# Silu of the gate rewritten with tanh, at steps of its own, in an attention and feed-forward kernel

## Chip, cores and metric
One core of a Trainium2 chip runs the whole program. The metric is the device time of one execution in microseconds (us); lower is better.

## What is computed
Inputs are x (4 batches of 1024 tokens, width 256), the attention weights Wq, Wk, Wv, Wo and the feed-forward weights w1, w2 with biases. Cut to what matters:

```python
xn = _layernorm(x, axis=-1)
s = _L0_attn_ref(xn, Wq, Wk, Wv, Wo)      # 16 heads of 16, 8 key heads, causal,
                                          # last 128 tokens or a landmark token
g = _silu(_L0_ffn_ref(xn, w1, b1, w2, b2))
# _L0_ffn_ref: h = gelu(xn @ w1_q.T + b1); h @ w2_q.T + b2, with w1_q, w2_q in {-1, 0, 1}
x = x + s * g
```

With z the output of the feed-forward part, the gate is silu(z) = z / (1 + exp(-z)) = z/2 (1 + tanh(z/2)).

## The kernel before
The program is written engine by engine, with semaphores set by hand. After a setup come five turns: one that only prepares batch 0, then one for each batch ("turn 0" to "turn 3"; `turn` in the code). Turns 0 to 2 do the attention of their batch and also prepare the next batch (`prep`); turns 1 to 3 first finish the second half of the batch before (`prev`).

A turn walks through 48 steps (`STEPS`). A step is one block of 128 keys (`kb`) for one group of 4 heads (`g`) and one chunk of 512 queries (`c`): 4 groups of 4 steps for chunk 0 (steps 0 to 15), 4 groups of 8 for chunk 1 (steps 16 to 47; `C1` is 16). In step i:
- PE does `scores(i, 0)`, `values(i - 2)`, `scores(i, 1)` (lines 735 and 742 for the scores and their mask, 755 for the values). `scores(i, u)` waits until the exponentials of step i - 1, half u, are done.
- ACT does `exps(i)`: for each half one or two exponentials from PSUM to the tile probs (lines 829 and 832), 128x1024 when the block lies before the diagonal.
- DVE copies out a finished group (`group_out`), and does the small work.

Between the steps stand jobs, in an order that the list `jobs_of` fixes by step numbers; each engine walks the same list and does its part. `ffn_up` is 8 blocks of the first feed-forward product (PE, line 672), each followed by a gelu on ACT into the tile `hid` (line 790) and by a split into h_hi and h_lo on DVE and POOL (lines 899, 904, 867). Those of chunk 1 stand just before step 16, those of the next batch's chunk 0 at the turn's end. `ffn_down` (PE, line 682) is spread over steps 6 to 13 and 34 to 41; its output plus bias is written by DVE to the tile `gate` (line 911, the "z add"; semaphore z_done). `out_proj` (PE, line 690) at steps 27 to 32, and at steps 4 and 5 of the next turn, is multiplied with the gate by DVE (line 919), and POOL adds x (line 863). `mean_row` (line 714) and `transpose` (line 696) prepare the next batch at steps 16 to 18; `v_proj` (line 709) stands at the turn's end, and ACT copies it out (line 806).

`gates(c)` on ACT (line 818) turns z into the gate in place: one Silu over 128x1024 for a chunk. It stands ahead of `exps(16)` for chunk 0, and behind the gelus at the turn's end for chunk 1:

```python
act.wait_ge(z_done, TC * (c + 1))
act.activation(gate[:, :, :], gate[:, :, :], ACT.Silu).then_inc(gate_done, 1)
```

Exp, Gelu and Silu each make the compiler place an ACT_TABLE_LOAD when the one before was of another kind. The first 1024 columns of `hid` also serve as `x_prev`, in which the second half of the batch before gets its residual at steps 4 and 5 and from which it is sent out.

Of the kernel before, what the change touches and what calls it, by code (L numbers as in the profile page):

```python
# [9 lines left out]
ALU = mybir.AluOpType  # L30
ACT = mybir.ActivationFunctionType
# [11 lines left out]
TC = CH // P  # L43


def kernel_program(nc, x, Wq, Wk, Wv, Wo, w1, b1, w2, b2, out):
# [5 lines left out]
    FT = F // P  # L52
# [36 lines left out]
    with ExitStack() as ctx:  # L89
# [3 lines left out]
        def sem(name):  # L93
# [67 lines left out]

        x_prev = hid[:, :, :].rearrange("p a n -> p (a n)")[:, 0:TC * D].rearrange("p (t d) -> p t d", d=D)
        head_block = x_prev[:, 0, 0:P]
        w_tmp = probs[:, 2].rearrange("p a n -> p (a n)")
# [27 lines left out]
            sem(n) for n in ("att_out", "att_in", "rden_done", "rden_in", "attT_done"))  # L192
        hid_split, hi_done, hid_split_pool, z_done, gate_done, prod_done, y_done, xres_in, y_out = (
            sem(n) for n in ("hid_split", "hi_done", "hid_split_pool", "z_done", "gate_done", "prod_done", "y_done", "xres_in", "y_out"))
        xprev_in, w_first = sem("xprev_in"), sem("w_first")
# [306 lines left out]
        DOTS_AT, RANK_AT = 6, 19  # L502
        LN_AT = 5

        def jobs_of(main, prep, prev):
# [33 lines left out]
        def turn(b, main, prep, prev, x_next):  # L539
# [30 lines left out]
            with nc.Block(no_gpsimd_drain=True) as block:  # L570
# [207 lines left out]
                def _(act):  # L778
                    def job(n, kind, *a):
                        bank, before_it = bank_of[n]  # L780
                        ps = aux_ps[:, bank, :]
                        if kind == "ffn_up":
                            c, f, u = a
                            act.wait_ge(aux_done, n + 1)
                            if u >= NHID:

                                act.wait_ge([hid_split, hid_split_pool][(u - NHID) % 2], (u - NHID) // 2 + 1)
                            if u == 0 and prev:
                                act.wait_ge(y_out, 16)
                            act.activation(hid[:, u % NHID, :], ps, ACT.Gelu, bias=b1_sb[:, f:f + 1]).then_inc(aux_free[bank], 1)  # L790
# [24 lines left out]
                    def gates(c):  # L815

                        act.wait_ge(z_done, TC * (c + 1))
                        act.activation(gate[:, :, :], gate[:, :, :], ACT.Silu).then_inc(gate_done, 1)

# [16 lines left out]
                    for i in range(NSTEP if main else last_step + 1):  # L836
                        for j in jobs_at(i - 0.5, i):
                            job(*j)
                        if main and i == C1:
                            gates(0)  # L840
                        if main:
                            exps(i)
                        for j in jobs_at(i, i + 0.5):
                            job(*j)
                    if main:
                        tail = jobs_at(NSTEP - 0.5, 999)
                        first = [j for j in tail if j[1] == "ffn_up"]
                        for j in first:
                            job(*j)
                        gates(1)  # L850
                        for j in tail[len(first):]:
                            job(*j)
# [24 lines left out]
                def _(dve):  # L877
# [14 lines left out]
                    def job(n, kind, *a):  # L892
# [21 lines left out]
                        elif kind == "out_proj":  # L914
                            t, u = a
                            dve.wait_ge(aux_done, n + 1)
                            if u >= n_prev and t % TC == 0:
                                dve.wait_ge(gate_done, t // TC + 1)
                            dve.tensor_tensor(gate[:, t % TC, :], ps[:, 0:D], gate[:, t % TC, :], ALU.mult).then_inc(prod_done, 1)  # L919
                            dve.wait_ge(prod_done, u + 1)  # L920
# [33 lines left out]
                        elif kind == "dilate":  # L954
                            dve.wait_ge(aux_done, n + 1)
                            dve.tensor_scalar(landmark[:, :], ps[:, 0:T], 1.0, None, ALU.min).then_inc(aux_free[bank], 1)
                            dve.wait_ge(aux_free[bank], before_it + 1)

                    def normalise_x(t):
# [72 lines left out]
                    for i in range(last_step + 1 if not main else NSTEP + LAG):  # L1032
# [4 lines left out]
                        if main:  # L1037
# [7 lines left out]
                            if i == C1 + 8:  # L1045
                                normalise_heads(own)
                            if not prep and i == GROUP_END[5] + LAG + 4:
                                reciprocals(own + 1)
# [56 lines left out]
```

## Time and profile before
| what | value |
|---|---|
| median of 3 runs (lowest, highest) | 742.63 us (741.88, 743.72) |
| span of the profiled execution | 740.2 us |
| PE busy | 632.2 us (85%) |
| PE weight loads busy | 357.2 us (48%) |
| DVE busy | 374.9 us (51%) |
| ACT busy | 475.4 us (64%) |
| POOL busy | 88.3 us (12%) |
| mean granted clock of PE | 0.922 |

The span is from the first to the last instruction of one profiled execution; the page gives no other time for it. The median of the runs is 2.4 us above that span. Busy shares are over the whole span; the granted clock is a share of full speed (1.00 is 2.4 GHz, 0.50 is 1.2 GHz).

### The profile page before, as it was taken

The page shows a single profiled execution, that of the slowest core. Times are in us where ns is not written, and L with a number is a line of the kernel's source. Part 1 is how long each engine was busy: PE and PEld are TensorE (multiplying, and loading weights), DVE is VectorE, ACT ScalarE, POOL GpSimd, SP SyncE. Part 2 cuts the span into 40 slices and gives each one's busy share as a digit, 9 for nine tenths or more (in the row PEclk, how much of TensorE's full clock was granted, in tenths as well). Part 3 has the DMA queues.
Part 4 walks back from the last instruction along what each step waited for, and adds up shares of the span by engine and source line. Part 5 has one row for each costly group of instructions (what it writes and reads, how often), then busy time and mean ns, then how long its engine had stood idle before and what let it go on. Part 6 is the DMA issues. An engine that isn't in the chain of part 4 may idle for free. (4 is left out here: it accounts for less than half of the span.)

```text
span 740.2 us, 11752 instructions
## 1 busy us (share of the span) xinstructions
PE 632.2 (85%) x4336; PEld 357.2 (48%) x4336; DVE 374.9 (51%) x1000; ACT 475.4 (64%) x723; POOL 88.3 (12%) x94
## 2 busy tenths in 40 slices
PE   1226866999999979999999769999999899799982
PEld 1215752664455456554454636654554556334532
DVE  4976972574827444676545615748364521410101
ACT  1021245678776866687778655697768656888680
POOL 5600020020010021020100201110100210201001
PEclk9656776999999999999999969999999799899996
DMA  7000298200127359001091748001082690020101
GB/s 213 0 0 1 40 115 135 43 8 9 58 36 94 53 79 203 20 7 31 30 107 31 95 130 113 12 8 57 23 108 40 83 157 15 8 89 8 51 10 49
DMA packets 46833, 43.84 MB, mean 59 GB/s; under 512 B 6065, under 2 KB 41394, under 8 KB 46770
## 3 DMA queue, kind: packets, MB, share of 16 engines
q1 hardware_dynamic: 44642, 41.18, 33.4%
q10 hardware_dynamic: 2128, 1.84, 0.8%
q8 instruction: 38, 0.62, 0.4%
q14 instruction: 25, 0.20, 0.1%
HBM read 11.28 MB, written 4.19 MB: 21 GB/s over the span
## 5 line engine op out<-in xcount | busy, mean ns | idle before, releaser
L829 ACT ACTIVATE probs<-sc_ps,shift 128x512 f32<-128x512 f32 (+1 forms) x288 | 175.6, 616 | 98.7 <-PE sc_ps L742 98.0
L735 PE MATMUL sc_ps<-q_stack,k_stack 99*128 99x512 bf16 (+3 forms) x768 | 197.3, 342 | 29.3 <-PEq L209 10.2
L832 ACT ACTIVATE probs<-sc_ps,key_bias 128x1024 f32<-128x1024 f32 (+3 forms) x256 | 204.6, 817 | 16.9 <-PE sc_ps L735 16.3
L755 PE MATMUL att_ps<-probs,v_sb 128*32 128x512 f32 (+3 forms) x1536 | 165.6, 503 | 0.0
L735 PEld LDWEIGHTS sc_ps<-q_stack,k_stack 99*128 99x128 bf16 x768 | 49.9, 99 | 177.2 <-ACT probs L832 65.0
L742 PE MATMUL sc_ps<-near_mask,mask_ident 128*128 128x256 bf16 (+1 forms) x576 | 103.8, 264 | 0.0
L867 POOL TENSOR_TENSOR h_lo<-hid,h_hi 128x512 fp32r<-128x512 f32 x32 | 43.1, 1347 | 338.4 <-DVE h_hi L899 338.4
L742 PEld LDWEIGHTS sc_ps<-near_mask,mask_ident 128*128 128x128 bf16 x576 | 55.7, 101 | 36.8 <-issue 6.7
L682 PE MATMUL aux_ps<-w2T,h_hi 128*128 128x256 f32 x256 | 70.1, 307 | 0.0
L682 PE MATMUL aux_ps<-w2T,h_lo 128*128 128x256 f32 x256 | 63.2, 279 | 0.0
L790 ACT ACTIVATE hid<-aux_ps,b_sb 128x512 f32<-128x512 f32 x64 | 43.0, 687 | 22.5 <-PE aux_ps L672 14.7
L672 PE MATMUL aux_ps<-xT_hi,w1T 128*128 128x512 f32 x128 | 54.8, 428 | 2.7 <-ACT hid L790 2.7
L899 DVE CAST h_hi<-hid 128x512 fp32r<-128x512 f32 x64 | 30.7, 492 | 45.0 <-ACT hid L790 44.8
L755 PEld LDWEIGHTS att_ps<-probs,v_sb 128*32 128x32 f32 x1536 | 30.4, 108 | 47.3 <-issue 31.3
L672 PE MATMUL aux_ps<-xT_lo,w1T 128*128 128x512 f32 x128 | 51.3, 401 | 0.0
L911 DVE TENSOR_TENSOR gate<-aux_ps,b_bc 128x256 f32<-128x256 f32 x32 | 13.6, 424 | 73.7 <-PE aux_ps L682 53.0
L1013 DVE COPY att_raw<-att_ps 128x512 f32<-128x512 f32 x32 | 22.1, 691 | 56.4 <-PE att_ps L755 34.8
L682 PEld LDWEIGHTS aux_ps<-w2T,h_hi 128*128 128x128 f32 x256 | 48.1, 188 | 1.9
L682 PEld LDWEIGHTS aux_ps<-w2T,h_lo 128*128 128x128 f32 x256 | 48.4, 189 | 0.3
L919 DVE TENSOR_TENSOR gate<-aux_ps,gate 128x256 f32<-128x256 f32 x32 | 13.6, 424 | 59.6 <-PE aux_ps L690 59.6
L690 PE MATMUL aux_ps<-wo_sb,attT 128*128 128x256 f32 x128 | 34.3, 403 | 10.3 <-DVE attT L1025 10.3
L863 POOL TENSOR_TENSOR xn<-xn,gate 128x256 f32<-128x256 f32 x20 | 14.6, 729 | 221.7 <-DVE gate L919 221.5
(152 smaller groups left out, 776.8 us busy)
## 6 DMA issues: line engine op xcount, KB each, us to landing
q_stack<-q_parts SPq DMA_DIRECT2D x96, 128.0 KB, 8.2
k_stack<-k_parts SPq DMA_DIRECT2D x24, 256.0 KB, 8.8
xn<-in_L_attn_hidden_states SPq DMA_DIRECT2D x4, 1024.0 KB, 9.2
attT<-att_raw SPq DMA_DIRECT2D x128, 32.0 KB
rden_bc<-den SPq DMA_DIRECT2D x64, 64.0 KB
probs<-in_L_ffn_w SPq DMA_DIRECT2D x2, 1024.0 KB, 7.7
out_y<-xn SPq DMA_DIRECT2D x4, 512.0 KB, 6.5
xn<-in_L_attn_hidden_states SPq DMA_DIRECT2D x3, 512.0 KB, 4.0
```

Of the source, the lines that this page charges most:

```text
L672: last = pe.matmul(ps, w1T[:, k, f * P:(f + 1) * P], part[:, k, c * CH:(c + 1) * CH], start=(k == 0 and part is xT_hi), stop=(k == KD - 1 ...
L682: last = pe.matmul(ps[:, 0:D], part[:, f, q * P:(q + 1) * P], w2T[:, f, :], start=(f == 0 and part is h_hi), stop=(f == FT - 1 and part is ...
L690: last = pe.matmul(ps[:, 0:D], attT[:, k, q * P:(q + 1) * P], wo_sb[:, k, :], start=(k == 0), stop=(k == KD - 1))
L735: last = pe.matmul(sc_ps[:, 2 * u + hh, lo:CH], k_stack[0:KROWS + SHIFT_ROWS, h // REP, kb * P:(kb + 1) * P], q_stack[0:KROWS + SHIFT_ROWS ...
L742: last = pe.matmul(sc_ps[:, 2 * u + hh, lo:near], mask_ident[:, :], near_mask[:, first:end:kb + 1, :], start=False, stop=True)
L755: last = pe.matmul(att_ps[32 * q:32 * q + 32, n % 2, lo:CH], v_sb[:, kb, j * VW:j * VW + 32], probs[:, i % 3, q, lo:CH], start=(kb == 0), ...
L790: act.activation(hid[:, u % NHID, :], ps, ACT.Gelu, bias=b1_sb[:, f:f + 1]).then_inc(aux_free[bank], 1)
L829: last = act.activation(probs[:, i % 3, us, lo:near], sc_ps[:, us, lo:near], ACT.Exp, bias=shift[:, 0:1], scale=HD ** -0.5)
L832: last = act.activation(probs[:, i % 3, us, near:CH], sc_ps[:, us, near:CH], ACT.Exp, bias=key_bias[:, kb:kb + 1], scale=HD ** -0.5)
L867: pool.tensor_tensor(h_lo[:, f, :], hid[:, u % NHID, :], h_hi[:, f, :].bitcast(F32), ALU.subtract).then_inc(hid_split_pool, 1)
L899: ins = dve.tensor_copy(h_hi[:, f, :], whole)
L1013: dve.tensor_copy(att_raw[:, :], att_ps[:, n % 2, :]).then_inc(att_out, 1)
```

## The change
The Silu becomes a tanh of z/2 on ACT into the first 1024 columns of hid (`half_tanh`), and a product (1 + tanh) * z on DVE; the factor 1/2 is applied where the out-projection is multiplied with the gate. Both stand at steps of their own: the tanh of chunk 0 before `exps(14)`, that of chunk 1 before `exps(44)`, and the products one step later on DVE. The first gelu of each block waits for the product, since it overwrites hid. The wait for the output DMA of x_prev moves from the first gelu to the first tanh.

```diff
+        half_tanh = hid[:, :, :].rearrange("p a n -> p (a n)")[:, 0:TC * D].rearrange("p (t d) -> p t d", d=D)
...
+        GATES_AT = (14, C1 + 28)
...
-                            if u == 0 and prev:
-                                act.wait_ge(y_out, 16)
+                            if main and u % FT == 0:
+
+                                act.wait_ge(gate_done, u // FT + 1)
...
                     def gates(c):
 
                         act.wait_ge(z_done, TC * (c + 1))
-                        act.activation(gate[:, :, :], gate[:, :, :], ACT.Silu).then_inc(gate_done, 1)
+                        if c == 0 and prev:
+                            act.wait_ge(y_out, 16)
+                        act.activation(half_tanh[:, :, :], gate[:, :, :], ACT.Tanh, scale=0.5).then_inc(tanh_done, 1)
...
-                        if main and i == C1:
+                        if main and i == GATES_AT[0]:
                             gates(0)
+                        if main and i == GATES_AT[1]:
+                            gates(1)
...
-                        for j in first:
-                            job(*j)
-                        gates(1)
-                        for j in tail[len(first):]:
+                        for j in first + tail[len(first):]:
                             job(*j)
...
-                            dve.tensor_tensor(gate[:, t % TC, :], ps[:, 0:D], gate[:, t % TC, :], ALU.mult).then_inc(prod_done, 1)
+                            dve.scalar_tensor_tensor(gate[:, t % TC, :], ps[:, 0:D], 0.5, gate[:, t % TC, :],
+                                                     ALU.mult, ALU.mult).then_inc(prod_done, 1)
...
+                    def gates(c):
+
+
+                        dve.wait_ge(tanh_done, c + 1)
+                        dve.scalar_tensor_tensor(gate[:, :, :], half_tanh[:, :, :], 1.0, gate[:, :, :],
+                                                 ALU.add, ALU.mult).then_inc(gate_done, 1)
...
+                            if i == GATES_AT[0] + 1:
+                                gates(0)
+                            if i == GATES_AT[1] + 1:
+                                gates(1)
```

ACT around the chunk boundary of turn 3, before (`probs` is written by an exponential, `hid` by a gelu, `gate` by the Silu):

```order
L829 ACTIVATE probs<-sc_ps,shift 128x2x256
L832 ACTIVATE probs<-sc_ps,key_bias 128x2x128
L829 ACTIVATE probs<-sc_ps,shift 128x2x256 x2
L829 ACTIVATE probs<-sc_ps,shift 128x2x128 x2
L790 ACT_TABLE_LOAD
L790 ACTIVATE hid<-aux_ps,b_sb 128x512 x8
L818 ACT_TABLE_LOAD
L818 ACTIVATE gate<-gate 128x1024
L832 ACT_TABLE_LOAD
L832 ACTIVATE probs<-sc_ps,key_bias 128x1024 x6
```

And with the change, at the same place (line 803 is the tanh, 773 the gelu, 814 and 817 the exponentials):

```order
L814 ACTIVATE probs<-sc_ps,shift 128x2x256
L817 ACTIVATE probs<-sc_ps,key_bias 128x2x128
L803 ACTIVATE hid<-gate 128x1024
L814 ACTIVATE probs<-sc_ps,shift 128x2x256 x2
L814 ACTIVATE probs<-sc_ps,shift 128x2x128 x2
L773 ACT_TABLE_LOAD
L773 ACTIVATE hid<-aux_ps,b_sb 128x512 x8
L817 ACT_TABLE_LOAD
L817 ACTIVATE probs<-sc_ps,key_bias 128x1024 x6
```

The tanh stands between the exponentials of steps 13 and 14 with no table load, and between gelus and exponentials one load is left of two. ACT at step 44 of turn 3 with the change:

```order
L817 ACTIVATE probs<-sc_ps,key_bias 128x2x384
L803 ACTIVATE hid<-gate 128x1024
L814 ACTIVATE probs<-sc_ps,shift 128x2x256
L817 ACTIVATE probs<-sc_ps,key_bias 128x2x256
L814 ACTIVATE probs<-sc_ps,shift 128x2x256
```

Before, the two exponentials of 128x2x384 and 128x2x256 (steps 43 and 44) followed each other. DVE at step 15 of a turn that prepares a batch, with the change (line 948 is the product, 883 the cast of the first gelu's output):

```order
L895 TENSOR_TENSOR gate<-aux_ps,b_bc 128x256
L1005 COPY att_raw<-att_ps 128x512
L953 TENSOR_SCALAR xn<-xn,mv,rstd 128x256 x2
L956 SCALAR_TENSOR_TENSOR resid,ssq<-xn 128x256 x2
L948 SCALAR_TENSOR_TENSOR gate<-hid,gate 128x1024
L883 CAST h_hi<-hid 128x512
L888 TENSOR_TENSOR h_lo<-hid,h_hi 128x512
L883 CAST h_hi<-hid 128x512 x2
```

The product stands alone between the normalisation of x and the first cast of the gelu block, where nothing stood before.

## Rows read from the trace of the kernel before
**Rows 1.** Groups of ACT: line, operation, count | busy us, mean ns | idle before
```profile
L818 ACT ACT_TABLE_LOAD x8 | 10.3, 1283 | 0.1
L818 ACT ACTIVATE gate<-gate 128x1024 f32<-128x1024 f32 x8 | 8.5, 1059 | 0.1
```
**Rows 2.** Timeline of ACT, boundary of turn 3: start us, us, instruction, count [idle before]
```profile
636.64 1.27 ACT L790 ACTIVATE hid<-aux_ps,b_sb 128x512 f32<-128x512 f32 x2 [0.94 <-POOL h_lo L867]
637.92 1.28 ACT L818 ACT_TABLE_LOAD   x1
639.22 1.06 ACT L818 ACTIVATE gate<-gate 128x1024 f32<-128x1024 f32 x1
...
641.59 2.12 ACT L832 ACTIVATE probs<-sc_ps,key_bias 128x1024 f32<-128x1024 f32 x2
```
**Rows 3.** Timeline of PE at the same place
```profile
642.75 1.03 PE L735 MATMUL sc_ps<-q_stack,k_stack 99*128 99x512 bf16 x2 [4.25 <-ACT probs L832]
```
**Rows 4.** Windows: busy us (count) by engine, granted clock of PE, DMA share, GB/s
```profile
642.00:643.00 1.00, 0.25 (x1) 0.13 (x2) 0.00 (x0) 1.00 (x2) 0.00 (x0) 0.60 0.00 0
...
649.00:650.00 1.00, 1.00 (x9) 0.35 (x10) 0.59 (x1) 0.93 (x1) 0.00 (x0) 0.98 0.01 2
...
723.00:724.00 1.00, 0.00 (x0) 0.00 (x0) 0.00 (x0) 0.00 (x0) 0.00 (x0) 1.00 0.18 41
```
**Rows 5.** Timeline of ACT in turn 3: step 19, then steps 24 to 27
```profile
650.08 0.47 ACT L829 ACTIVATE probs<-sc_ps,shift 128x256 f32<-128x256 f32 x1
...
660.30 5.17 ACT L832 ACTIVATE probs<-sc_ps,key_bias 128x1024 f32<-128x1024 f32 x5
...
666.71 0.47 ACT L829 ACTIVATE probs<-sc_ps,shift 128x256 f32<-128x256 f32 x1
```
**Rows 6.** Boundary of turn 0: timeline of PE and ACT, and one window
```profile
165.56 3.62 PE L714 MATMUL aux_ps<-xn,ones 128*128 128x256 f32 x16
...
168.88 5.13 ACT L832 ACTIVATE probs<-sc_ps,key_bias 128x1024 f32<-128x1024 f32 x5
174.24 1.11 ACT L832 ACTIVATE probs<-sc_ps,key_bias 128x1024 f32<-128x1024 f32 x1 [0.22 <-PE sc_ps L735]
...
168.00:172.00 4.00, 3.92 (x30) 2.56 (x28) 2.50 (x4) 3.99 (x5) 0.44 (x1) 1.00 0.00 0
```
**Rows 7.** Timeline: ACT at the end of turn 0, PE at the program's end
```profile
266.82 0.78 ACT L806 ACTIVATE v_sb<-aux_ps 128x128 f32<-128x128 f32 x4 [1.78 <-PE aux_ps L709]
...
730.17 5.34 PE L690 MATMUL aux_ps<-wo_sb,attT 128*128 128x256 f32 x14 [10.28 <-DVE attT L1025]
```
**Rows 8.** Timeline of ACT and PE, steps 44 and 45 of turn 0
```profile
244.59 0.69 ACT L829 ACTIVATE probs<-sc_ps,shift 128x512 f32<-128x512 f32 x1
245.16 0.70 ACT L832 ACTIVATE probs<-sc_ps,key_bias 128x512 f32<-128x512 f32 x1
...
246.06 0.48 PE L735 MATMUL sc_ps<-q_stack,k_stack 99*128 99x384 bf16 x2
```
**Rows 9.** Timeline of DVE, ACT and PE, steps 13 to 16 of turn 0
```profile
152.31 0.43 DVE L911 TENSOR_TENSOR gate<-aux_ps,b_bc 128x256 f32<-128x256 f32 x1 [1.58 <-PE aux_ps L682]
152.75 0.69 ACT L829 ACTIVATE probs<-sc_ps,shift 128x512 f32<-128x512 f32 x1 [0.41 <-PE sc_ps L742]
154.03 0.28 PE L735 MATMUL sc_ps<-q_stack,k_stack 99*128 99x128 bf16 x2
155.58 0.47 ACT L829 ACTIVATE probs<-sc_ps,shift 128x256 f32<-128x256 f32 x1 [0.29 <-PE sc_ps L742]
158.15 0.43 DVE L899 CAST h_hi<-hid 128x512 fp32r<-128x512 f32 x1 [3.06 <-ACT hid L790]
```
**Rows 10.** Groups of DVE, columns as in rows 1
```profile
L1025 DVE TENSOR_TENSOR attT<-attT,rden_bc 128x1024 f32<-128x1024 f32 (+1 forms) x9 | 10.0, 1107 | 31.8 <-DMA rden_bc<-den 31.5
L919 DVE TENSOR_TENSOR gate<-aux_ps,gate 128x256 f32<-128x256 f32 x32 | 13.6, 424 | 59.6 <-PE aux_ps L690 59.6
L964 DVE SCALAR_TENSOR_TENSOR resid<-xn 128x256 f32<-128x256 f32 x32 | 12.3, 423 | 0.6
```

More of the change, by code:

```diff
@@ L192, in kernel_program @@
             sem(n) for n in ("att_out", "att_in", "rden_done", "rden_in", "attT_done"))
-        hid_split, hi_done, hid_split_pool, z_done, gate_done, prod_done, y_done, xres_in, y_out = (
-            sem(n) for n in ("hid_split", "hi_done", "hid_split_pool", "z_done", "gate_done", "prod_done", "y_done", "xres_in", "y_out"))
+        hid_split, hi_done, hid_split_pool, z_done, gate_done, tanh_done, prod_done, y_done, xres_in, y_out = (
+            sem(n) for n in ("hid_split", "hi_done", "hid_split_pool", "z_done", "gate_done", "tanh_done", "prod_done", "y_done", "xres_in", "y_out"))
         xprev_in, w_first = sem("xprev_in"), sem("w_first")
```

## The prediction, made before the changed kernel had been run
> **What bounds the kernel now.** I read the page first: PE is busy for 85% of the span and ACT for 64%, so ACT as a whole is not the bound, and only places where the two engines hand work to each other can matter. The second view is the grouped instructions of ACT: 8 Silu instructions of 1.06 us, each with a table load of 1.28 us of its own [rows 1]. Together with what they force (the load that brings the exponential back) this is what the change touches. The third view is the timeline, read at the four kinds of place where a Silu stands now or a tanh will stand: the chunk boundary (step 16) in the turns that prepare the next batch, the same in the last turn, the end of a turn, and the new steps 14 and 44. In what follows "turn 0" to "turn 3" are the four turns with attention.
>
> **The boundary in turn 3** is the one place where the Silu is exposed. The last two gelus end at 637.91, then come load, Silu, load, and the first exponential starts at 641.59, 3.67 us after the first load began [rows 2]. PE stands still for 4.25 us on that exponential [rows 3]. It costs twice: the granted clock is 0.60 in the mean of the microsecond from 642, then half, and is back only in the one from 649 (0.98) [rows 4]. At 1.2 GHz PE can't keep up with ACT: from the first exponential of step 16 to the first of step 19, six of the 1024-wide kind, it takes 650.08 - 641.59 = 8.49 us. The same six at 2.4 GHz, one head group later and again with no other work between, take 666.71 - 660.30 = 6.41 us [rows 5].
>
> **The boundary in turns 0 to 2** looks the same on ACT, but PE has other work there: the mean row (16 matmuls, 3.62 us from 165.56) and the transposes for the next batch. PE is busy for 3.92 of the 4 us from 168 to 172. ACT, released by its last load, starts at 168.88, does five exponentials without a gap, and at 174.24 is again waiting for PE (0.22) [rows 6]. So the Silu is hidden under PE's own queue.
>
> **The end of a turn**: the Silu of the second chunk stands between the gelus and the copies of v. The second group of v copies waited 1.78 us for PE [rows 7], so that Silu is hidden too. In turn 3 it runs while PE sits out 10.28 us for the last attention group's DMA round trips [rows 7].
>
> **What is removed.** Eight loads and eight Silus. The listing of ACT shows no load ahead of a tanh, so 8 x 1.28 = 10.3 us of loads go [rows 1]. Only those of the turn 3 boundary are on the path: 3.67 us there becomes one load with its 1.30 us to the next start (637.92 to 639.22) [rows 2], so **-2.37 us**. The other seven Silus and loads were hidden and give 0; the cover is PE's 3.62 us of mean row plus transposes in three of them, and PE's v projection or the DMA chain in four. With the exponential 2.37 us earlier PE idles 4.25 - 2.37 = 1.9 us. Does the clock fall then? In the trace it stays at 1.00 until 724 at the program's end although PE stopped shortly before 720 [rows 4, 7], so it outlived some 4 us of idleness there, and it fell at the boundary only near the end of a stop of 4.25 us. I take it as kept: 8.49 - 6.41 = **-2.08 us**. Bounds: 0 (it falls all the same) and -2.1 (it stays).
>
> The Trainium skill, ScalarE: Activation LUTs, section What ACT_TABLE_LOAD costs, puts a switch of table sets at about 1283 ns of load and about 1380 ns of drain. The trace doesn't agree with the second part: the load starts 0.01 us after the last gelu's end and the Silu 1.30 us after the load's start [rows 2]. By the page the turn 3 boundary would win 1.36 us more; by the row it wins nothing more.
>
> **What is added on ACT.** A tanh of 128x1024 has no row. The nearest is the Silu of the same tile, 1.06 us; back-to-back instructions overlap by 0.12 us (0.69 us from 244.59, next start 245.16) [rows 1, 8], so it holds the exponentials up by 0.95 us. Ends: 0.69 us (the 512-wide exponential) and 1.06.
>
> Step 44: ACT has no gap there. The first pair of step 44 starts at 244.59, at once behind step 43, and ends at 245.86; PE's first scores of step 45, which wait for that, start at 246.06 [rows 8]. The slack is 0.20 us. PE then goes from scores to values to scores without a wait that could absorb it, and the gelus at the turn's end start from ACT's last exponential. So 0.95 - 0.20 = 0.75 us in each of 4 turns: **+3.0 us**. Ends 0 and 0.95 each.
>
> Step 14: the tanh needs the last z add, which ends at 152.74 on DVE; until then ACT was free. With the tanh first, the exponential of step 14 starts about 153.75 instead of 152.75, 1.0 us later. PE's scores of step 15 wait for its end, 153.44 before, 154.44 after, and stood at 154.03 [rows 9]. That is 0.41 us, and all behind it (values, scores, the gelus' table load, the gelu block) is back to back. 4 turns: **+1.6 us**. Ends 0 and 1.0 each.
>
> **What is added on DVE.** Eight products of 128x1024. No row shows this one; the 128x1024 product of attT takes 1.1 us in the mean [rows 10], so some 9 us of busy time. At step 15 DVE is idle for 3.06 us before the first gelu's cast at 158.15 [rows 9]; queued behind the product is just that cast, and the gelu itself, which now waits for the product (since the tanh uses the tile hid). The product can end near 156.3; ACT's last exponential ends at 156.05, the table load takes it to 157.3, and both come 0.4 later now [rows 1, 9]. At step 45 DVE has nothing but the cast behind the product either, and that waits for the gelus of the turn's end. Cost 0 at both, up to 1.1 us a turn if that cover were gone. The out-projection's product becomes scalar_tensor_tensor: 0.424 us now, against 0.423 for that operation on the same shape [rows 10]: 0. The wait for the output DMA moves from the gelu (step 16) to the tanh (step 14); that DMA is issued once the residuals of steps 4 and 5 are done, nine steps earlier, so 0. POOL and SP keep their order.
>
> **Sum** against the profiled execution (740.2): 3.0 + 1.6 - 2.37 - 2.08 = +0.15, so a span of about 740.4. The three runs have a median of 742.63, 2.4 us above that span; with the same distance **742.8 us**. What a measurement of this kernel can tell from no change is about 0.3%, 2.2 us: from 740.4 to 744.9 is "the same". The three runs alone lie 1.8 us apart, which is of the size of the clock's cold stretches at the start of a turn.
>
> **The rivals.**
> - *The clock falls all the same* (slower). PE's stop at the turn 3 boundary is cut from 4.25 to 1.9 us, not removed, and nothing in the trace has a stop of that length at full clock to compare. From the point at which 1.9 us is enough to lose it, the 2.08 us stay lost: 744.9. For it: the granted clock did fall before the 4.25 us were over. Against: the program's end. 0.14.
> - *The product holds the gelus.* If DVE's product ends after ACT's last exponential of step 15 (156.05) by more than the delay, load and gelus start later, and the whole gelu block with them: up to 1.1 us in each of 4 turns, 747.2. It needs the normalisation of x ahead of it on DVE to run later than it did. 0.05.
> - *The tanhs are absorbed* (faster). If gaps of ACT like the 0.41 and 0.29 us of steps 14 and 15 [rows 9] took them up at both places, +4.6 becomes some +1.6 and the time 739.8. Against: PE waits for ACT there, the gaps are PE's lateness handed on. 0.10.
> - *The Silu was exposed at every boundary.* Then 3 x 2.37 more: 735.7. For it: the three loads and Silus in a row on ACT. Against: PE's full windows [rows 6]. 0.06.
> - *A switch costs a drain as well.* As a mechanism of this kernel: were the activation ahead of a load to give its result up only after a drain that the rows don't show, the boundary of turn 3 would win about as much again as one load, 1.3 us: 741.5. 0.05. This is the page's rule above.
> - That the change doesn't do what it says (a load still stands before the tanh) is excluded by the listing.
>
> **How the numbers follow.** The forecast has 0.60, its own range is 741.3 to 744.4 (the ends of one term moved at a time, and the spread of runs). The time is its value, 742.8. The range reaches to the absorbed tanhs below and the lost clock above: 739.6 to 745.2; outside are the exposed Silus and the held gelus. Faster: 0.10 + 0.06 + 0.02 of the forecast = 0.18. Slower: 0.14 + 0.05 + 0.02 = 0.21, where the lost clock lies on the bound. Same: 0.61.
>
> **What would show it.** In the changed profile: 18 table loads instead of 26. At turn 3's boundary one load and then an exponential, PE idle about 1.9 us there, and the granted clock at 1.00 through the next 8 us. From the gelus' table load at the boundary to that at the turn's end turns 0 to 2 take 0.75 us more than before; from the last z add ahead of step 14 to the boundary's load 0.4 more. The copies of v still wait for PE, and longer. I am wrong if the stretch from step 16 to step 43 in turns 0 to 2 gets shorter by more than 0.3 us, if PE's scores of step 45 don't move against step 43, or if the clock in turn 3 falls.

## The result and the profile after

| | before | after |
|---|---|---|
| median of the runs (lowest, highest) | 742.25 us (741.25, 743.72), 4 runs | 748.77 us (746.29, 750.03), 4 runs |
| span of the profiled execution | 740.2 us | 746.7 us |
| ACT busy | 475.4 us | 464.9 us (62%) |
| DVE busy | 374.9 us | 384.5 us (51%) |
| PE busy | 632.2 us | 629.4 us (84%) |
| mean granted clock of PE | 0.922 | 0.936 |

The ratio is 1.008, 95% interval 1.0059 to 1.0102: 6.5 us slower, where 742.8 was forecast and 745.2 was the upper end. The engine that was relieved did get 10.5 us of its work off (475.4 to 464.9), TensorE ran at a slightly higher clock, and the program is longer. A second and larger comparison (e6 below, 12 runs against 23) put the ratio at 1.0045 (1.0024 to 1.0065). Both intervals lie above 1; the first four runs and the profiled execution lie at the dear end of what the changed kernel does. One execution in the comparisons below, e3's fifth, took 3265 us and is in no ratio.

The groups of the new instructions, columns as in [rows 1] (of ACT, then of DVE):

```profile
L773 ACT ACT_TABLE_LOAD x8 | 10.3, 1283 | 0.1
L803 ACT ACTIVATE hid<-gate 128x1024 f32<-128x1024 f32 x8 | 8.4, 1055 | 3.7 <-DVE gate L895 3.7
...
L903 DVE SCALAR_TENSOR_TENSOR gate<-aux_ps,gate 128x256 f32<-128x256 f32 x32 | 13.6, 424 | 60.3 <-PE aux_ps L672 60.3
L948 DVE SCALAR_TENSOR_TENSOR gate<-hid,gate 128x1024 f32<-128x1024 f32 x8 | 9.8, 1226 | 5.5 <-ACT hid L803 5.3
```

The tanh costs what the Silu cost (1055 against 1059 ns), the out-projection's product is unchanged (424 ns, [rows 10]). The product (1 + tanh) z takes 1226 ns, a little over the 1.1 us that was taken. New is the last column of the tanh: ScalarE stood idle for 3.7 us ahead of it, waiting for VectorE's z add.

**Cutting the time at marks.** To see where 6.5 us come from I cut both traces at the same instructions: the first exponential's table load of a turn ("start"), the turn's first z add, at step 7 ("z1"; the expectations below call it the z add of tile 1), the gelus' table load at the boundary, the gelus' table load at the turn's end, and in turn 3 the exponential's load at the boundary and the end. Each entry is the difference of two start times. The last two columns are second profiles of the same two kernels (e5, e6).

| stretch, us | before | after | before again | after again |
|---|---|---|---|---|
| start to z1, turns 0 / 1 / 2 / 3 | 19.29 / 21.18 / 28.15 / 22.68 | 20.51 / 21.06 / 29.37 / 22.91 | 19.34 / 21.16 / 29.87 / 23.35 | 20.54 / 20.97 / 29.07 / 22.71 |
| z1 to the boundary's load, turns 0 / 1 / 2 / 3 | 19.97 / 19.98 / 19.98 / 20.04 | 20.40 / **23.49** / 20.40 / 20.41 | 19.98 / 19.99 / 19.99 / 20.05 | 20.40 / **21.26** / 20.40 / 20.40 |
| boundary's load to that of the turn's end, turns 0 / 1 / 2 | 96.40 / 96.41 / 96.41 | 97.01 / 97.03 / 97.03 | 96.42 / 96.41 / 96.42 | 96.99 / 97.02 / 96.99 |
| turn 3: boundary's load to the exponential's | 11.45 | 9.10 | 11.45 | 9.08 |
| turn 3: from there to the end | 99.91 | 99.42 | 98.06 | 101.52 |

Of the 6.5 us, the boundary of turn 3 gives back 2.35. Step 14 takes 0.43 + 0.42 + 0.37 in turns 0, 2 and 3 and **3.51 in turn 1**. Step 44 takes 0.61 + 0.62 + 0.62 in turns 0 to 2, and in turn 3 it lies within the last line, whose sum is -0.49. From a turn's end load to the next start it is +0.25 in sum. The rest, +2.55 us, lies in the first line, ahead of any tanh. Of that last item turn 2's 1.2 us are not the change's: the kernel before, profiled again, shows 29.87 us there instead of 28.15, and 93.72 in sum instead of 91.30. The profile on which the prediction was built was a lucky one there. Turn 0's 1.2 us are another matter: the second profiles repeat them (19.34 against 20.54), although they lie ahead of the turn's first tanh. What sets them is open; it is not the work nearby, since e8 and e10 (below), which differ only by matmuls in turn 3, have 19.38 and 20.77 (e12, the same kernel as e10, 20.59).

The windows of that stretch show how it moves. Of turn 2, before and then before again (columns: busy us of PE, its weight loads, DVE, ACT, POOL, then PE's granted clock, DMA share, GB/s):

```profile
424.52:452.67 28.15, 21.38 (x146) 11.58 (x147) 6.46 (x15) 14.86 (x25) 2.91 (x4) 0.77 0.67 124
```

```profile
424.81:454.68 29.87, 22.85 (x146) 11.96 (x147) 6.47 (x15) 14.88 (x25) 2.91 (x4) 0.73 0.70 134
```

It is the same 146 matmul rows in 21.4 us or in 22.9 us of PE, with a mean granted clock of 0.77 or 0.73.

**Turn 1** is the finding of this trace. DVE first, at step 9 and at the last z add:

```profile
302.74 0.69 DVE L1005 COPY att_raw<-att_ps 128x512 f32<-128x512 f32 x1 [3.90 <-DMA den<-att_raw]
...
311.30 0.42 DVE L895 TENSOR_TENSOR gate<-aux_ps,b_bc 128x256 f32<-128x256 f32 x1
```

Then ACT at step 14, PE at step 15, and two windows behind it, all of the same execution:

```profile
311.76 1.06 ACT L803 ACTIVATE hid<-gate 128x1024 f32<-128x1024 f32 x1 [2.54 <-DVE gate L895]
...
313.45 0.28 PE L717 MATMUL sc_ps<-q_stack,k_stack 99*128 99x128 bf16 x2 [2.37 <-ACT probs L814]
...
313.00:314.00 1.00, 0.55 (x8) 0.36 (x12) 0.96 (x4) 0.97 (x2) 0.00 (x0) 0.80 0.11 23
314.00:315.00 1.00, 1.00 (x8) 0.08 (x8) 0.96 (x3) 0.47 (x1) 0.00 (x0) 0.50 0.19 43
```

DVE's copy of the second attention group has to wait until the DMAs of the first group have read the one tile att_raw. It waits 3.90 us. Behind it on DVE stand the layer norm's root, the normalisation of x and two z adds; DVE hardly pauses from there on, and the last z add starts 18.33 us behind z1 (311.30 - 292.97) where the trace of before has 16.20 (306.93 - 290.73). The tanh waits for it, all exponentials of step 14 wait behind the tanh, PE stands for 2.37 us, and on top the granted clock falls at 313.6, 2.5 us after PE had stopped. The kernel before had the same wait (1.37 us in this turn, 2.38 in its second profile), and nobody on ACT needed z before step 16.

Step 44 in turn 0, timeline of ACT:

```profile
246.21 1.05 ACT L803 ACTIVATE hid<-gate 128x1024 f32<-128x1024 f32 x1
247.15 0.69 ACT L814 ACTIVATE probs<-sc_ps,shift 128x512 f32<-128x512 f32 x1
```

The exponential comes 0.94 us behind the tanh's start (0.95 was taken), and 0.61 to 0.62 us of it reach the turn's end.

**Turn 3's boundary**, as [rows 2 to 4]: timeline of ACT, of PE, and windows.

```profile
646.00 1.27 ACT L773 ACTIVATE hid<-aux_ps,b_sb 128x512 f32<-128x512 f32 x2 [0.96 <-POOL h_lo L851]
647.28 1.28 ACT L817 ACT_TABLE_LOAD   x1
648.58 4.13 ACT L817 ACTIVATE probs<-sc_ps,key_bias 128x1024 f32<-128x1024 f32 x4
...
656.40 0.47 ACT L814 ACTIVATE probs<-sc_ps,shift 128x256 f32<-128x256 f32 x1
...
649.74 0.61 PE L717 MATMUL sc_ps<-q_stack,k_stack 99*128 99x512 bf16 x2 [1.90 <-ACT probs L817]
...
651.00:652.00 1.00, 0.60 (x3) 0.13 (x2) 0.46 (x1) 1.00 (x2) 0.00 (x0) 0.76 0.00 0
652.00:653.00 1.00, 1.00 (x6) 0.20 (x8) 0.00 (x0) 0.82 (x2) 0.00 (x0) 0.50 0.15 33
...
655.00:656.00 1.00, 1.00 (x10) 0.52 (x12) 0.27 (x1) 0.61 (x1) 0.00 (x0) 1.00 0.03 8
```

One load instead of two and the Silu; PE idle for 1.90 us, as forecast. But the granted clock falls to half all the same, at 651.5, 3.7 us after PE had stopped (it was busy again by then), and is back at 654.9. The six wide exponentials take 656.40 - 648.58 = 7.82 us, not 6.41.

### The profile page after: what moved, and what is told of

It is laid out like the page before. It is cut to its first block and busy times, and to the rows that moved or that the text cites. A ratio compares the mean times of both kernels' runs of the same rounds, so it can differ in the third digit from the quotient of the medians.

```text
span 746.7 us, 11756 instructions
## 1 busy us (share of the span) xinstructions
PE 629.4 (84%) x4336; PEld 351.8 (47%) x4336; DVE 384.5 (51%) x1008; ACT 464.9 (62%) x715; POOL 87.7 (12%) x94
## 5 line engine op out<-in xcount | busy, mean ns | idle before, releaser
L737 PE MATMUL att_ps<-probs,v_sb 128*32 128x512 f32 (+3 forms) x1536 | 167.8, 509 | 0.0
L883 DVE CAST h_hi<-hid 128x512 fp32r<-128x512 f32 x64 | 33.5, 538 | 36.3 <-ACT hid L773 35.8
L903 DVE SCALAR_TENSOR_TENSOR gate<-aux_ps,gate 128x256 f32<-128x256 f32 x32 | 13.6, 424 | 60.3 <-PE aux_ps L672 60.3
```

The source lines that it names most:

```text
L737: last = pe.matmul(att_ps[32 * q:32 * q + 32, n % 2, lo:CH], v_sb[:, kb, j * VW:j * VW + 32], probs[:, i % 3, q, lo:CH], start=(kb == 0), ...
L883: ins = dve.tensor_copy(h_hi[:, f, :], whole)
```

## The experiments

Theory A: the added time sits at the two tanhs (0.4 us at step 14, 0.6 at step 44, each four times), plus VectorE's lateness, which step 14 puts on the path in turn 1. The rivals: B, it is only how the cold clock falls at the turns' starts; C, step 14 or 44 costs more than its row says. All ratios are against runs of the kernel before on the same chip; a difference in us is the ratio's times the median of before there (743.1 to 743.7).

### e1 and e2: each half of the change alone

```diff
 e1: chunk 0 as before the change, chunk 1 with tanh
-                        if main and i == GATES_AT[0]:
-                            gates(0)
+                        if main and i == C1:
+                            silu(0)
 e2: chunk 1 as before the change, chunk 0 with tanh
-                        if main and i == GATES_AT[1]:
-                            gates(1)
...
                        for j in first:
                            job(*j)
+                        silu(1)
```

> Chunk 0 has its Silu back at the boundary, only the tanh at step 44 and its product stay. Theory A (the added time comes from the two places where a tanh stands ahead of an exponential, and of these mostly from step 14): step 44 costs 0.62 us in each of 4 turns as in the trace of the changed kernel, so +2.5 us against before, about 744.8, and the way from a turn's start to the boundary's gelu load is as before. Rival B (the added time is the clock's cold stretches at the starts of turns, which any change of phase moves): a time anywhere from 741 to 749, with differences sitting ahead of step 9 and not at the tanh. Rival C (step 44 is the costly place by something the trace does not show): over +4 us.

> Only the tanh at step 14 and its product stay, chunk 1 has its Silu back at the turn's end. Theory A: what is left of the changed kernel's +6.5 us without 4 x 0.62, so +4.0 us against before, about 746.3, with the last z add and the tanh in turn 1 late by some 2.5 us. Rival C: under +2.5 us. Theory A also asks that this one and e1 add up to the whole change within 1 us; rival B gives no such sum.

Measured: **e1 746.32 us, ratio 1.0035 (1.0017 to 1.0054)**, +2.6 us as expected; **e2 743.87, ratio 1.0007 (0.9997 to 1.0017)**, +0.5 us where +4.0 was expected. Boundary to turn's end is 97.02, 97.04 and 97.03 us in e1 and 96.40, 96.40 and 96.39 in e2; z1 to the boundary's load is 19.98 three times and 20.05 in e1, and 20.39 to 20.40 in all four turns of e2. So both prices stand exactly where theory A has them, and e2 misses its number mainly because its profile lacks the 3 us of turn 1: its DVE waited 0.22 us there for something else and not for the DMA. The two add to +3.1 us, less than the +6.5 of the first comparison. Rival B is half right: e1 has 94.6 us in its four starts and e2 95.4, with no tanh near them.

### e3: VectorE's wait taken away

```diff
+        def raw_of(n):
+            return hid[:, 2, :] if n == 1 else att_raw[:, :]
...
-                        if n >= 1:
+                        if n >= 2:
                             dve.wait_ge(att_in, 16 * (NQ + 1) * n)
-                        dve.tensor_copy(att_raw[:, :], att_ps[:, n % 2, :]).then_inc(att_out, 1)
+                        dve.tensor_copy(raw_of(n), att_ps[:, n % 2, :]).then_inc(att_out, 1)
```

> The changed kernel, but the second attention group's copy out of PSUM goes to a free third of hid instead of att_raw, so that VectorE doesn't wait there for the DMA that reads the first group's copy. Theory A (the tanh of turn 1 is late because VectorE, in order, stands behind that DMA): VectorE's wait of 3.9 us at step 9 of turn 1 goes, the z adds come in time, and the stretch to the boundary's load falls by some 2.5 to 3 us in turn 1 and by little elsewhere: about 746 us. Rival D (the z adds wait for TensorE's ffn_down sums, not for this DMA): no change, 748.8. Rival B: turn 1 keeps its extra 3 us ahead of step 9.

Measured: 747.91 us, ratio 1.0062 (1.0033 to 1.009). In its trace z1 to the boundary's load is 20.40, 20.41, 20.40 and 20.40 us: turn 1 is like the others, and no wait for the DMA is left at step 9. The missing wait is the edit's doing and not luck, as the table below lets one see: the transfers ahead of the first group's landed later than in e6 (6.70 us behind z1 against 6.35), where DVE waited 2.63 us. The total doesn't show a gain over the changed kernel (e6, 1.0045); the intervals overlap, and in this profile the stretch from turn 3's exponential load to the end took 101.65 us (99.42 in after). By total time e3 is inconclusive, and its number, 746, was missed.

The traces of the other kernels settle the mechanism, since each is one more sample of that wait in turn 1. The second column tells where the wait comes from: it is when the last of the 12 transfers into q_stack, which the turn's start issues, has landed, in us behind z1. The transfers that read att_raw stand behind them and the output's transfer in the same queue.

| kernel | last q_stack transfer landed | DVE's wait for the DMA | last z add behind z1 | tanh at step 14? | z1 to the boundary's load |
|---|---|---|---|---|---|
| e12 | 3.57 | none | 16.20 | no | 19.98 |
| before | 5.24 | 1.37 | 16.20 | no | 19.98 |
| e1 | 5.98 | 2.05 | 16.49 | no | 19.98 |
| before again (e5) | 6.39 | 2.38 | 16.83 | no | 19.99 |
| e8 | 7.18 | 3.54 | 17.98 | no | 19.99 |
| e2 | 3.36 | none | 16.20 | yes | 20.39 |
| e3 (copy to another tile) | 6.70 | none | 16.20 | yes | 20.40 |
| after again (e6) | 6.35 | 2.63 | 17.07 | yes | 21.26 |
| after | 7.85 | 3.90 | 18.33 | yes | 23.49 |

VectorE has some 1.76 us to spare: the last z add is late by the wait less that (2.38 - 1.76 = 0.62, and 16.83 - 16.20 = 0.63; 3.90 - 1.76 = 2.14, and 2.13). Without a tanh at step 14 a late z costs nothing (e8, late by 1.77 us), with it it costs all of it, and in the worst case the clock as well. The late z is probably in part the other side of a gain: where turn 1's start was short (21.0 to 21.4 us) and the copy was not moved, DVE waited 1.4 to 3.9 us, and where it was long (21.8 to 23.1 us), 0 to 1.6 us, in all thirteen such profiles.

### e4 and e9: the tanh ahead of the gelus

```diff
 e4
-                        if main and i == GATES_AT[0]:
-                            gates(0)
...
                         if main:
                             exps(i)
+                        if main and i == C1 - 1:
+                            gates(0)
 e9: the same, and the tanh of chunk 0 written to rden_bc, which is idle then
-                            if main and u % FT == 0:
-                                act.wait_ge(gate_done, u // FT + 1)
+                            if main and u == FT:
+                                act.wait_ge(gate_done, 2)
```

> The changed kernel, but the chunk 0 tanh stands behind the exponentials of step 15, just ahead of the gelus' table load, and the product follows it. Theory A: the z adds are done by then in every turn, so the wait for them goes and the tanh costs its bare 0.95 us four times: turn 1 falls by 2.5 us, turn 3 rises by 0.4, and the sum is 4 x 0.95 + 4 x 0.62 - 3.0 (turn 3's boundary) = +3.3 us against before, about 745.6. The product (1.23 us) is covered by the table load (1.28 us). Rival E (the product holds the gelus): one further us in each turn, 749.6. Rival B: no relation to where the tanh stands.

> e4 with the chunk 0 tanh written to rden_bc instead of hid, so that no gelu waits for the product (the tanh still stands behind the exponentials of step 15). In e4 the gelus' table load, which carries the gelu's wait, stood 1.41 us for the product in each turn, and the gelu block then took 10.28 us to the exponential's load instead of 9.09. Rival E of e4 (the product holds the gelus): both go, 4 x (1.41 + 1.2) = -10.4 us against e4's +14.8, so about +4 us against before; from the z add of tile 1 to the boundary's load 20.9 us in every turn, turn 1 too, however late VectorE is. The other reading (a tanh just ahead of the gelus starves TensorE by itself): over +8 us.

Measured: **e4 758.54 us, ratio 1.0203 (1.0179 to 1.0226)**, +15 us where I had written +3.3; **e9 747.23, ratio 1.0047 (1.0033 to 1.0062)**, +3.5. The two timelines of ACT, e4 and then e9:

```profile
157.13 1.05 ACT L803 ACTIVATE hid<-gate 128x1024 f32<-128x1024 f32 x1
159.58 1.28 ACT L773 ACT_TABLE_LOAD   x1 [1.41 <-DVE gate L948]
```

```profile
156.25 1.05 ACT L803 ACTIVATE rden_bc<-gate 128x1024 f32<-128x1024 f32 x1
157.31 1.28 ACT L775 ACT_TABLE_LOAD   x1
```

In e4 the gelu's wait for the product sits on the table load that goes with the gelu, so the load can't cover the product, as I had assumed. ACT loses 1.41 us, PE runs dry, and its clock halves in the middle of the gelu block; windows of e4:

```profile
160.00:161.00 1.00, 0.00 (x0) 0.00 (x0) 0.00 (x0) 0.99 (x2) 0.00 (x0) 1.00 0.00 0
...
163.00:164.00 1.00, 1.00 (x4) 0.78 (x3) 0.10 (x2) 0.69 (x1) 0.84 (x1) 0.50 0.06 16
```

With a tile of its own all of it goes: z1 to the boundary's load is 20.91, 20.93, 20.93 and 20.99 us, 0.95 over the kernel before, in turn 1 too, where DVE had waited 1.59 us (within the 1.76 us to spare, so this run doesn't test a late z).

### e5 and e6: both kernels again

> The kernel before, profiled once more. From the six traces so far: from the z add of tile 1 to the boundary's gelu load every turn takes 19.98 to 20.04 us without a tanh and 20.39 to 20.41 with one, but from a turn's start to that z add it took 19.3 to 20.6 us in turn 0 and 28.2 to 29.8 in turn 2, whatever the kernel. Theory A2: those starts vary from run to run of one kernel by the clock's cold stretch, so here turn 0 and turn 2 need not repeat the 19.29 and 28.15 us of the first trace. Rival F: they belong to the kernel before (its code without a tanh), so they repeat within 0.2 us.

> The changed kernel again, against as many runs of before as the others had. Theory A2: its steady costs are 4 x 0.41 (step 14) + 4 x 0.62 (step 44) - 2.35 - 0.67 (turn 3's boundary) = +1.1 us, and on top of that only what turn 1 adds in those runs where the DMA holds VectorE up; e1 and e2 add to +3.1. So +3 to +5 us, 747 to 749, and the wait for the tanh's z in turn 1 anything from 0.4 to 3 us. Rival C: +6.5 us again with turn 1 at 23.5 us from the z add of tile 1 to the boundary's load.

Measured: e5 742.81 us (one run); **e6 746.73, ratio 1.0045 (1.0024 to 1.0065)**, +3.3 us, at the low end of what was expected. Their stretches stand in the table above. Turn 2's start is 29.87 us in e5, so rival F falls for it; turn 0's repeats (19.34), as F has it, but e1 has 20.39 there and e4, with both tanhs, 19.40, so neither tanh's presence decides it. The half clock at turn 3's boundary differs as well: the six wide exponentials take 8.49 us before and 7.20 in e5, 7.82 after and 8.21 in e6. Whether PE stood for 4.25 or for 1.90 us does not decide it.

### e7: two tanhs at step 44

```diff
 e1, and
                         if main and i == GATES_AT[1]:
                             gates(1)
+                            act.wait_ge(tanh_done, 1)
+                            act.activation(half_tanh[:, :, :], gate[:, :, :], ACT.Tanh, scale=0.5).then_inc(tanh_done, 1)
```

> e1 with the tanh of step 44 done twice (the second waits for the first's semaphore). Theory A: step 44 has no slack left, so the second costs its whole time, 1.05 us and the hand-over, in each of 4 turns: +4.2 to 4.8 us over e1, some 750.8; from the boundary's gelu load to the turn's end gelu load 98.1 to 98.2 us instead of 97.02. Rival G (the 0.62 us is a step of some other kind, such as a lost slot of TensorE's order, that a longer stay does not raise in proportion): under +0.5 us a turn.

Measured: 751.64 us, ratio 1.0116 (1.0086 to 1.0147), +8.6 us, 6.0 over e1 where 4.2 to 4.8 was expected. Boundary to turn's end is 98.10, **99.69** and 98.11 us: 1.08 more than e1 for the second tanh in turns 0 and 2, as expected, and 2.65 in turn 1. In each of these turns PE stood for 1.74 us behind the tanhs; in turn 1 the clock fell, in turns 0 and 2 it stayed at 1.00. PE and two windows of turn 0, then of turn 1:

```profile
248.85 0.50 PE L717 MATMUL sc_ps<-q_stack,k_stack 99*128 99x384 bf16 x2 [1.74 <-ACT probs L820]
...
249.00:250.00 1.00, 1.00 (x12) 0.36 (x10) 0.00 (x0) 1.00 (x3) 0.00 (x0) 1.00 0.00 0
250.00:251.00 1.00, 1.00 (x12) 0.36 (x5) 0.00 (x0) 0.89 (x2) 0.00 (x0) 1.00 0.00 0
...
407.21 0.50 PE L717 MATMUL sc_ps<-q_stack,k_stack 99*128 99x384 bf16 x2 [1.74 <-ACT probs L820]
...
409.00:410.00 1.00, 1.00 (x5) 0.13 (x2) 0.00 (x0) 0.25 (x1) 0.00 (x0) 0.50 0.00 0
410.00:411.00 1.00, 1.00 (x5) 0.60 (x4) 0.00 (x0) 0.00 (x0) 0.00 (x0) 0.50 0.00 0
```

### e8: the tanh where ACT waits anyway

The listing of ACT shows no table load between gelu and tanh either, so the tanh can stand within the gelu block. Chunk 0's goes ahead of the seventh gelu, where ACT waited for POOL; chunk 1's goes to the Silu's old place.

```diff
+        half_tanh = rden_bc[:, :, :].rearrange("p a n -> p (a n)").rearrange("p (t d) -> p t d", d=D)
...
                         if kind == "ffn_up":
                             c, f, u = a
+                            if main and c == 1 and f == FT - 2:
+                                gates(0)
...
                         for j in first:
                             job(*j)
+                        gates(1)
...
+                            if i == C1 + 3:
+                                gates(0)       (the product, on DVE)
```

> Tanh shares the gelu's table set as well as the exponential's (the listing of ACT shows no load on either side of it). So the chunk 0 tanh stands between the sixth and seventh gelu, where ScalarE waited 1.01 us (0.94 in turn 3) for POOL's h_lo, writes to rden_bc, and its product is done at step 19; the chunk 1 tanh stands behind the turn's last gelu, where the Silu was. Theory A: nothing is paid at steps 14 and 44, the tanh costs 0.05 to 0.1 us in the gap, and turn 3's boundary wins 2.35 + 0.67 us: -2.7 us against before, some 741. Rival H (the gap is needed, or the product at step 19 holds the transposes or the k projection): 0 to +4 us.

Measured: 742.83 us, ratio 0.9987 (0.9966 to 1.0007), -1.0 us where -2.7 was expected: faster is not shown. The timeline of ACT in turn 0 and of PE in turn 3:

```profile
162.75 0.69 ACT L774 ACTIVATE hid<-aux_ps,b_sb 128x512 f32<-128x512 f32 x1 [0.24 <-PE aux_ps L654]
163.34 1.05 ACT L802 ACTIVATE rden_bc<-gate 128x1024 f32<-128x1024 f32 x1
164.44 1.27 ACT L774 ACTIVATE hid<-aux_ps,b_sb 128x512 f32<-128x512 f32 x2
165.73 1.28 ACT L816 ACT_TABLE_LOAD   x1
...
643.47 0.60 PE L717 MATMUL sc_ps<-q_stack,k_stack 99*128 99x512 bf16 x2 [1.88 <-ACT probs L816]
```

The tanh took the place of the 1.01 us wait, and the boundary's load to that of the exponential is 9.17 us against 9.15 for the gelus alone before. z1 to the boundary's load is back at 19.97 to 20.05 us, boundary to turn's end at 96.40 to 96.43. All that the change cost at steps 14 and 44 is gone, its 2.35 us stay. But PE's stop of 1.88 us still cost the clock: 0.50 through 647 and 648, and 7.61 us for the six exponentials.

### e10, e11 and e12: PE kept busy through its stop

```diff
+                jobs += [(C1, "fill")]
...
+                        elif kind == "fill":
+                            for _ in range(4):        (9 in e11)
+                                last = pe.matmul(ps[:, 0:D], ones[:, :], wo_sb[:, 0, :], start=True, stop=True)
```

> e8 with 4 idle matmuls (128x256 f32, result unused) on TensorE behind the scores of step 16 in turn 3, 1.8 us of its 1.88 us stop. Theory K (it is this stop that lets the granted clock fall some 4 us later): the clock stays at 1.00 through the 10 us after it, and from the exponential's load to the end 1 to 2 us go, so -2 to -3 us against before, 740.5. Rival L (the clock falls for the stops of 0.4 us between ACT-bound exponentials that follow): the half clock shows for 3 to 5 us as in e8, time as e8.

> The kernel before with 9 such idle matmuls in turn 3's stop of 4.25 us (4.07 us), nothing else. Theory K: the clock stays at 1.00 behind the boundary, the six wide exponentials take some 6.4 to 6.9 us instead of 8.49, and the kernel is 1 to 2 us faster than before: the whole of the clock term of the prediction, without a tanh. Rival L: the half clock shows all the same, 0 us.

> e10 once more, since its interval ends only 0.16% below the kernel before. Theory K and the placement among the gelus: steadily -2.35 us (turn 3's load and Silu) and -0.8 to -2.1 us (half clock behind its stop), so a ratio of 0.994 to 0.997 again, the six wide exponentials behind turn 3's boundary in 6.4 us again, and 19.98 us from the z add of tile 1 to the boundary's load. Rival M (the first result was the chance of the turns' starts): a ratio of 0.999 to 1.001.

Measured: **e10 742.02 us, ratio 0.9964 (0.9944 to 0.9984); e12, the same kernel, 741.55, ratio 0.9969 (0.995 to 0.9988)**; e11 742.66, ratio 0.9984 (0.9966 to 1.0002). PE and ACT at turn 3's boundary in e10, and one window of 10 us (each of the four matmuls is two in the trace):

```profile
643.81 1.89 PE L705 MATMUL aux_ps<-wo_sb,ones 128*128 128x256 f32 x8
645.86 0.60 PE L721 MATMUL sc_ps<-q_stack,k_stack 99*128 99x512 bf16 x2 [0.16 <-ACT probs L820]
...
644.69 5.13 ACT L820 ACTIVATE probs<-sc_ps,key_bias 128x1024 f32<-128x1024 f32 x5
...
651.06 0.47 ACT L817 ACTIVATE probs<-sc_ps,shift 128x256 f32<-128x256 f32 x1
...
643.00:653.00 10.00, 9.27 (x62) 3.49 (x54) 5.01 (x6) 9.74 (x12) 2.66 (x2) 1.00 0.07 15
```

The clock is 1.00 throughout and the six exponentials take 651.06 - 644.69 = 6.37 us; in e11, which is the kernel before with nothing but the idle matmuls, also 6.37. Theory K stands: PE's stop makes the clock fall, and the wait of 0.40 us behind it (at 647.87 in e10), which is still there, doesn't (rival L falls). Filled, the clock held in three profiles of three; unfilled, a stop of 1.65 to 4.25 us there lost it in eleven of eleven. e12's trace agrees: 1.00 throughout, 6.36 us. e10 and e12 are 2.7 and 2.3 us faster than the kernel before, as expected, and so faster than both kernels. e11's own gain, 1.2 us, is not shown by its interval, which just reaches 1.

## Why the prediction was wrong

- **Step 44** was right in mechanism and size: 0.61 to 0.62 us a turn against 0.75.
- **Step 14** was right where VectorE is in time: 0.42 us in turns 0 and 2, 0.37 in turn 3, against 0.41. *It failed in turn 1.* The sentence "until then ACT was free" and the price of 0.41 were read in turn 0 alone ([rows 9]) and multiplied by four. In turns 1 and 2 VectorE may have to wait for the DMA of the first attention group, and the z add is the last of a chain with 1.76 us to spare. The trace of before showed that wait (1.37 us in turn 1, 0.85 in turn 2). Cost in turn 1: 3.1 us above the 0.4 in the first profile (2.1 of late z; the rest goes with the half clock from 313.6), 0.9 in the second, nothing in e2. The rival "the product holds the gelus" named a late normalisation of x, but looked for its effect at the product; it came through the tanh.
- **The boundary's 2.37 us** were right: 2.35 in the first, 2.37 in the second pair of profiles. By the rule of the Trainium skill, ScalarE: Activation LUTs, section What ACT_TABLE_LOAD costs, it would have been more: an estimate from the page's drain of about 1380 ns beside the load gives about 1.36 us. Neither pair shows it.
- **"I take it as kept", -2.08 us for the clock, failed.** The 1.90 us stop cost the clock as the 4.25 us stop did. What came of it over the six wide exponentials is 0.67 us gained in the first pair (8.49 to 7.82) and 1.01 lost in the second (7.20 to 8.21). The row on which I rested it, full clock until 724 after PE had stopped, says that the clock falls late, not that it doesn't fall. The rival with the lost clock had 0.14 and should have been the forecast. As the rival would have it with 0.62 in place of 0.75, the sum is 4 x 0.62 + 4 x 0.41 - 2.37 = +1.8 us. Turn 1's lateness comes on top, 0 to 3.1 us, and turn 0's start, 1.2 us in both pairs; e6's +3.3 us lies within that, but how it is shared between them is not shown.
- **The product on DVE "cost 0"** held, but not with the margin given. In turn 0 it ended 156.31 + 1.23 = 157.54, and the table load started at 157.68. The text let the load's 1.28 us count as cover; e4 shows that the load waits too. The real margin was 0.14 us in turns 0 and 2.
- **The other seven Silus cost nothing**: in e8, which has no Silu and none of their loads, the stretches of turns 0 to 2 from z1 to the turn's end are those of before within 0.03 us, and from there to the next start it takes 17.23, 17.42 and 17.07 us against 17.09, 17.40 and 17.06.
- **The spread.** The sum was set against one profile of before whose four turn starts took 91.3 us. The thirteen profiles of this and the other kernels had 91.3 to 96.7, with 93.9 in the middle: the one of before is, with e9's, the shortest of all fourteen. A range of 3 us either side was narrow for that, even with every term right.

What stays open: how the first comparison came to 6.5 us and the second to 3.3. The marks explain the first pair of profiles in full (2.55 us in the starts, 3.1 us in turn 1), but how often turn 1 is that late was seen in two profiles of the changed kernel only. The second pair lies 4.7 us apart (741.1 and 745.8) for another reason, its last stretch, which is 3.46 us longer. Of these, 1.75 are half clock behind turn 3's boundary: from the exponential's load to the next head group's first wide exponential e5 takes 661.77 - 643.04 = 18.73 us and e6 664.76 - 644.28 = 20.48. Step 44 has 0.6, and 1.1 are the last 14 rows of the out-projection (4.70 and 5.82 us). Runs of one kernel lie up to 6 us apart and more (e8: 738.68 to 745.14), so one pair of spans doesn't tell a difference of this size; the stretches between the marks do.

## What to carry to other kernels

A price read in one turn of a loop holds for that turn: look at the same place in every turn, and ask of the operand that the moved instruction will need how late its engine is there, and behind which DMA. An instruction moved ahead of its old place is paid for by the slack of its producer, which cost nothing while nobody waited. Where an activation shares its table set with both neighbours, the place to look for is one where its engine waits anyway; and where a stop of TensorE can't be removed, a few idle matmuls in it can keep its clock up: the six wide exponentials went from 7.61 us in e8 to 6.37 in e10. How much of that the whole program gets is not clear of noise here (e11).

## What the runs showed of the hardware

- Tanh runs between exponentials and between gelus without a table load, while Silu between the same two had one on each side (1283 ns each).
- A semaphore wait written for the activation behind a table switch holds up the load itself (1.41 us in e4).
- A stop of PE of 1.7 to 1.9 us brought the granted clock from 2.4 to 1.2 GHz in some cases and not in others. The 1.9 us stop of turn 3 did in the profiles of after, e2, e3, e6, e8 and e9; the 1.74 us stop of e7 did in turn 1 and did not in turns 0 and 2. In the six of turn 3 the fall came 2.1 (e9) to 4.5 us (e8) after the stop began, when PE was busy again (in after: stop from 647.84, fall at 651.5), and half clock then lasted 3.4 (after) to 6.8 us (e6). Filled with idle matmuls, the same stop kept full clock in e10 and e12, and the 4.25 us stop of the kernel before did in e11.
